# Moving the Silu blocks of a two-layer sequence kernel to the fifteenth slot of their units, with the products, softplus and tap sums around them

## The reference, cut to what matters

```
xn = layernorm(x) * (1 + scale) + shift          # scale, shift from silu(c) @ ada_w
x_in, z = split(xn @ in_proj_w.T)                # 1024 channels each
u  = silu(causal_conv4(x_in) + conv_b)           # 4 taps along the sequence
dt_r, B, C = split(u @ x_proj_w.T)               # 64, 16, 16 columns
dt = softplus(dt_r @ dt_proj_w.T + dt_proj_b)
for t:  h = h * exp(dt[t] * A) + dt[t] * u[t] * B[t];  y[t] = sum_n h[.., n] * C[t, n]
x1 = x + gate * ((y + u * D) * silu(z)) @ out_proj_w.T
```

## Time and profile before

| | |
|---|---|
| time, median of 3 runs | 2797.12 us (2796.01 to 2797.8) |
| the profiled execution's own time | 2798.95 us |
| its span, first to last instruction | 2797.2 us |
| before the first scan | 102.7 us |
| first layer's scans, 102.7 to 2198.3 | 2095.6 us |
| the rest: end of layer 1, layer 2 | 598.9 us |
| busy share of the span | PE 83%, DVE 83%, ACT 54%, POOL 65% |
| granted TensorE clock, mean | 0.923 of full speed |
| transfers | 178.2 MB, mean 64 GB/s |

### The profile page before, as it was taken

How to read it: one execution, slowest core, us unless ns; L and a number is a source line. 1 busy time by engine, 2 the same in 40 slices (tenths; PEclk the granted TensorE clock), 3 DMA queues, 4 the chain that set the end, 5 groups by cost and what they waited for, 6 DMA issues and landing times. The chain is left out here.

```text
span 2797.2 us, 23766 instructions
## 1 busy us (share of the span) xinstructions
PE 2332.3 (83%) x6868; PEld 1183.7 (42%) x6868; DVE 2309.3 (83%) x2514; ACT 1519.9 (54%) x3034; POOL 1818.4 (65%) x1119
## 2 busy tenths in 40 slices
PE   6788888888887888798889878887887699888988
PEld 2223333333333333233333333333332278767876
DVE  2698899889989988898899889988999566675667
ACT  4556656665666566556655665666555233332333
POOL 0377878887888788788878887888876412132203
PEclk9889899899989899999999999989988899999999
DMA  5410041013103100311041013002100121021103
GB/s 191 181 49 23 15 151 42 23 54 124 34 23 108 70 30 23 136 42 61 18 151 42 23 46 132 27 23 95 68 27 0 59 68 52 18 102 55 38 16 106
DMA packets 79040, 178.18 MB, mean 64 GB/s; under 512 B 7421, under 2 KB 10749, under 8 KB 78910
## 3 DMA queue, kind: packets, MB, share of 16 engines
q1 hardware_dynamic: 78910, 176.66, 18.6%
HBM read 159.33 MB, written 17.30 MB: 63 GB/s over the span
## 5 line engine op out<-in xcount | busy, mean ns | idle before, releaser
L1147 POOL TENSOR_TENSOR arena<-arena 128x1024 f32<-128x1024 f32 x512 | 1199.8, 2353 | 395.0 <-ACT arena L492 394.1
L803 DVE TENSOR_TENSOR_SCAN arena<-ps,arena 128x512 f32<-128x512 f32 x1024 | 1247.6, 1249 | 48.4 <-ACT ps L492 48.4
L259 PE MATMUL ps<-arena,keep 128*128 128x512 f32 x1760 | 932.4, 663 | 233.4 <-POOL arena L1147 191.0
L492 ACT ACTIVATE ps<-arena 128x512 f32<-128x512 f32 x1088 | 724.4, 680 | 456.8 <-DVE arena L803 421.2
L791 DVE TENSOR_TENSOR arena<-ps,arena 128x1024 f32<-128x1024 f32 x512 | 614.3, 1200 | 107.2 <-ACT ps L492 106.9
L259 PEld LDWEIGHTS ps<-arena,keep 128*128 128x128 f32 x1760 | 349.5, 207 | 756.5 <-issue 364.5
L218 PE MATMUL ps<-arena 128*128 128x512 f32 x1024 | 469.9, 607 | 14.8 <-issue 13.4
L492 ACT ACTIVATE arena<-arena 128x2 f32<-128x2 f32 (+2 forms) x697 | 234.9, 339 | 158.8 <-POOL arena L1099 86.8
L218 PEld LDWEIGHTS ps<-arena 128*128 128x128 f32 x1024 | 199.8, 197 | 284.9 <-issue 283.4
L246 PE MATMUL ps<-arena 128*128 128x512 f32 x512 | 233.8, 599 | 7.2 <-issue 6.4
L1121 POOL TENSOR_TENSOR arena<-arena 128x512 f32<-128x512 f32 x168 | 220.4, 1312 | 7.0
(11 more groups left out here) (110 smaller groups left out, 2496.4 us busy)
## 6 DMA issues: line engine op xcount, KB each, us to landing
arena<-scr_bc SPq DMA_DIRECT2D x128, 512.0 KB, 7.5
arena<-in_inT SPq DMA_DIRECT2D x128, 256.0 KB, 2.7
arena<-in_x SPq DMA_DIRECT2D x17, 512.0 KB, 3.7
scr_x<-arena SPq DMA_DIRECT2D x32, 256.0 KB, 2.0
arena_b<-scr_x SPq DMA_DIRECT2D x16, 512.0 KB, 3.6
arena_c<-scr_x SPq DMA_DIRECT2D x32, 256.0 KB, 2.7
out<-arena_c SPq DMA_DIRECT2D x32, 256.0 KB, 2.1
arena<-in_x SPq DMA_DIRECT2D x30, 256.0 KB, 3.3
```

The costliest lines, as they stand in the source:

```text
L259: last = e.matmul(YP, ident, hb[G % R][:, i, :], start=False, stop=(g == NG - 1 and i == n - 1))
L492: return e.activation(o_, i_, f, **kw)
L803: e.tensor_tensor_scan(H, DA[s % 4], H, h0, MUL, ADD).then_inc(v_sc)
L1147: m_ = e.tensor_tensor(H, H, BC[:, 16 + GN * g:16 + GN * g + GN, :], MUL)
```

## The change

The Silu blocks move from slot 11 to slot 14 of their units (in unit 6 from slot 10 to slot 12). Around them these move too:

- `z_mm`: slots 8 and 9 to slots 8 and 10;
- `dt_mm`: 4 to 5; `softplus`: 6 to 7; `add`: 8 to 9; `du`: 9 to 10 (each a slot later, in all units). `du_copy` stays in slot 13, but its code now stands ahead of the Silu blocks;
- `x_mm` of block 2: (4, 0) to (3, 15); block 3: (4, 5) to (4, 2); block 4: (4, 13) to (4, 10); block 6: (5, 14) to (5, 15). Evacuations and taps follow at their fixed distances: the evacuations are then at (3, 2), (3, 6), (4, 2), (4, 5), (4, 13), (5, 4), (6, 2), (6, 5), the taps of blocks 2, 3, 4 and 6 at (4, 3) to (4, 5), (4, 6) to (4, 8), (4, 14) to (5, 0) and (6, 3) to (6, 5);
- `proj`: (6, 12) to (6, 14); `proj_evac`: (7, 1) to (7, 3); `store_bc`: (7, 2) to (7, 4).

No instruction's shape and none's number changes.

```diff
@@ -143,10 +143,10 @@
-        XMM = {(2, 15): 0, (3, 3): 1, (4, 0): 2, (4, 5): 3, (4, 13): 4, (5, 1): 5, (5, 14): 6, (6, 2): 7}
+        XMM = {(2, 15): 0, (3, 3): 1, (3, 15): 2, (4, 2): 3, (4, 10): 4, (5, 1): 5, (5, 15): 6, (6, 2): 7}
         XEV = {after(k, 3): i for k, i in XMM.items()}
         TAP = {after(k, 4 + w): (i, 2 - w) for k, i in XMM.items() for w in range(3)}
-        SILU = {(3, 11): (0, 2), (5, 11): (2, 5), (6, 10): (5, 8)}
+        SILU = {(3, 14): (0, 2), (5, 14): (2, 5), (6, 12): (5, 8)}
@@ -160,8 +160,8 @@
-                if j % 2 == 1 and pr in (8, 9) and U + 1 < NU:
-                    V = U + 1 + pr - 8
+                if j % 2 == 1 and pr in (8, 10) and U + 1 < NU:
+                    V = U + 1 + (pr - 8) // 2
                     WSEQ.append((V // 8, 8 + V % 8))
@@ -286,13 +286,13 @@
-                    if U + 1 < NU and pr == 4:
+                    if U + 1 < NU and pr == 5:
                         dt_mm(U + 1)
-                    if U + 1 < NU and j % 2 == 1 and pr in (8, 9):
-                        z_mm(U + 1 + pr - 8)
+                    if U + 1 < NU and j % 2 == 1 and pr in (8, 10):
+                        z_mm(U + 1 + (pr - 8) // 2)
                     if more and (j, pr) in XMM:
                         x_mm(c + 1, XMM[j, pr])
-                    if more and (j, pr) == (6, 12):
+                    if more and (j, pr) == (6, 14):
                         proj(c + 1)
@@ -631,7 +631,7 @@
-                if U + 1 < NU and pr == 6:
+                if U + 1 < NU and pr == 7:
                     softplus(U + 1)
@@ -639,7 +639,7 @@
-                if more and j == 7 and pr == 1:
+                if more and j == 7 and pr == 3:
                     proj_evac(c + 1)
@@ -647,8 +647,10 @@
+                if U + 1 < NU and pr == 13:
+                    du_copy(U + 1)
                 silu = False
-                if U + 1 < NU and j % 2 == 1 and pr == 11:
+                if U + 1 < NU and j % 2 == 1 and pr == 14:
                     z_silu(U + 1)
                     z_silu(U + 2)
                     silu = True
@@ -657,8 +659,6 @@
                 if silu:
                     e.preload_act_table_set("natural_log_exp_and_others")
-                if U + 1 < NU and pr == 13:
-                    du_copy(U + 1)
@@ -850,7 +850,7 @@
-                if U + 1 < NU and pr == 8:
+                if U + 1 < NU and pr == 9:
                     add(U + 1)
@@ -1134,7 +1134,7 @@
-                if U + 1 < NU and pr == 9:
+                if U + 1 < NU and pr == 10:
                     du(U + 1)
@@ -1295,7 +1295,7 @@
-                if more and (j, pr) == (7, 2):
+                if more and (j, pr) == (7, 4):
                     store_bc(c + 1)
```

## The result

The changed kernel takes 2802.46 us (median of 20 runs, 2796.98 to 2805.89) beside 2795.93 us (20 runs, 2793.74 to 2797.99) before: a ratio of 1.0022, 95% interval 1.0016 to 1.0029. It is slower by a fifth of a per cent, where 2773 us and "faster" were forecast. One execution of experiment 10 took 2988.82 us at a mean granted clock of 0.737 and is left out of that experiment's median and ratio.

A forecast was written before the change was run, and what follows sets the result against it. VectorE's work sets the pace, with time lost at the Silu blocks. Five steady chunks (-3.9 each) -19.5, chunk 0 +0.7, chunk 4 +1.9, chunk 7 -6.9: -23.8 us, giving 2773 us beside the 2797.12 median; range 2746 to 2800.

The forecast's parts named there:

- Step 1: Unit 3: expand waits for du alone, 4.7 us left; the unit begins its successor at 34.8 instead of 35.97, -1.2 us.
- Step 3: Unit 5: GpSimd's taps done early, the whole expand wait goes by a 0.4 us margin; 29.1 instead of 37.96, -8.9 us.
- step 4: Unit 6: repeats unit 4's pattern, silu_u still ahead of du_copy; 35.7 instead of 35.79 us, -0.1 us.
- Step 2: Unit 4: late state copy and closer evacuations delay GpSimd, ScalarE and TensorE; 35.3 instead of 29.04 us, +6.3 us.
- Step 5: The rest: dt_mm costs nothing, softplus's new place mostly pays for later du; unit 1 0.4 more, unit 0 0.4 less.
- The sum: All chunks: five steady ones -19.5, chunk 0 +0.7, chunk 4 +1.9, chunk 7 -6.9, together -23.8 us.
- (b): Rival: waits only move, du is late wherever the block was, unit 5 wins no more than unit 4 loses; 2797, chance 0.10.
- (c): Rival, slower: GpSimd carries its lateness from unit 4 into unit 5, so du ends late there; 2810, chance 0.13.
- (a): Rival: unit 4 finds cover, about half of its 6.3 us loss goes, 3.2 in each of seven chunks; 2751, chance 0.20.
- (d): Rival: each of a Silu block's two table switches takes twice its row, 2.6 us more behind du_copy; 2835, chance 0.01.

The follow-up runs named there:

- experiment 10: Changed kernel with du in slot 9, keep_state before the Silu block, old x_mm slots, unit 6's block in slot 14, chunk 0's embedding columns in unit 4: 2735.04 us.
- Experiment 8: Kernel before the change with only the step-size chain one slot later (dt product 5, softplus 7, add 9, du 10): 2800.92 us, ratio 1.0017.
- experiment 7: Kernel before the change with only the Silu blocks in slot 14 (12 in unit 6) behind du_copy and the projection two slots later: 2764.65 us, ratio 0.9884.
- Experiments 2: Changed kernel with keep_state of slot 14 ahead of the Silu block instead of behind it: 2788.42 us, ratio 0.997.
- experiment 3: Changed kernel with the eight transposes of slot (1, 15) done over three times in slot (2, 0) on TensorE: 2787.68 us, ratio 0.9964.
- experiment 1: Changed kernel with du on GpSimd back in slot 9 instead of slot 10: 2761.68 us, ratio 0.9877.
- experiment 5: Changed kernel with chunk 0's second embedding column product and its use on VectorE moved from unit 3 to unit 4: 2795.45 us, ratio 0.9997.

## Why the prediction was wrong

**Step 1, unit 3,** was right to the row: 34.8 us worked out, 34.82 measured, the first expand waiting 4.66 us where 4.7 was worked out, behind a `du_copy` that waits for L1127. **Step 3** was right too (29.1 and 29.12 us), with block 4's evacuation out of the way, and **step 4** nearly (35.7 and 36.1).

**Step 2, unit 4,** named the right mechanism and sized it 0.7 to 1.5 us too low (35.3 against 36.0 to 36.8 in the steady chunks). In chunk 5 the term is block 4's evacuation, "over at 63.5, so it costs nothing": it is over at 66.4, counted from the same moment, while `du` ends at 65.2 where 65.1 was worked out. Its product comes late, since TensorE has waited 4.14 us for GpSimd before it and does the sums ahead of it at the lower clock (four records in 3.78 us again), so the evacuation and not `du` sets the copy.

**Step 5 failed, and with it the sign.** It set units 0, 1 and 2 at no change: the `mul` brought forward by softplus' new place was said to pay "for most of the `mul` that `du` now lets pass", and TensorE's work to keep its cost. Units 0 and 1 grow by 0.7 and 0.5 us: the first `mul` after softplus does come 1.8 us sooner (GpSimd's idle time before it in unit 0 falls from 4.8 to 2.95 us), but the next one then waits 0.76 us for its own state copy, and `du`, a whole `mul` of 2.3 us later in the order, ends after VectorE has arrived. Experiment 8, the chain alone, gives units 0 and 1 the same growth (0.7 and 0.5 us), and experiment 7, the blocks without the chain, none. Unit 2 grows by 1.6 us in chunks 2, 3 and 6, by 3.0 in chunk 5, and not at all in chunk 1. That was priced at nothing because each pace was taken from rows at the higher clock; the state copy behind the block of unit 1 opens a gap of 3 us on TensorE, and where the granted clock falls behind it, the sums that `y_fin` needs are slow. The gap by itself adds nothing there (chunk 1). Experiments 2 and 3 take the fall away in chunks 1 to 6, experiment 3 by nothing but work that fills the gap, and experiment 1 in all but chunks 2 and 6. Over the eight chunks units 0 to 2 lose 22.9 us where nothing was forecast; by these sums the scan phase would otherwise have come out some 19 us shorter than before.

**The sum** for chunk 0 failed by 4.7 us: +0.7 was forecast, +5.4 came. Units 0 to 2 are 5.2 of the miss. Unit 3 is 3.1: it grew by 1.9 us where -1.2 was forecast, since the product that only this chunk has between the two z products was not followed through the two banks, though a later Silu frees a bank later. Undoing that tie wins some 7 us (experiment 5), more than the 3.1; the kernel before had the same tie. Units 5 and 7 came out better than forecast. In all, the scan phase came out 27.4 us above the forecast: 19.1 from the five steady chunks (3.8 each, of which units 0 to 2 are 2.8 in chunk 3 and unit 4 0.8), 4.7 from chunk 0, 2.8 from chunk 4, 0.8 from chunk 7.

**The rivals.** The result lies nearest to (b), 2797 us, and by half of its mechanism: `du`, a `mul` later, is late wherever the block stands (experiment 1). But unit 5 won all of its wait, more than unit 4 lost, and what made up the difference, units 0 to 2, is not in (b). (c) was wrong, GpSimd starts unit 5 in time. (a) and (d) were wrong: unit 4 found no cover, and the block of unit 3 takes 4.6 us with two table loads of 1.28 and no gap behind either. The range ended 2.5 us below the median.

**What cost what.** The new place of the Silu blocks is a gain, 31 us by itself. With it, VectorE waits for `du` itself instead of for the block. In the new order `du` alone a slot later costs 41 us; in the old order the whole chain a slot later costs 5. In unit 3 the two can be compared: the old order loses nothing by it (34.97 us in experiment 8, 35.97 before), the new one 3.7 (34.82 us in the changed kernel, 31.09 in experiment 7), since there the block no longer hides the lateness. The totals don't compare so simply, since the 5 us are a difference of larger gains and losses.

## What to carry to other kernels

Where a wait is taken away, the one that ends second sets the new time, so a step that moves in the same change must be priced behind the new wait and not behind the old: here `du`, one multiplication later on GpSimd, gave back more than the Silu block's move had won (41 and 31 us). Whoever puts a long block on an engine should look at the small copies that come behind it, since a 0.2 us state copy held up GpSimd for 3 us, and TensorE with it. An idle stretch on TensorE may cost nothing as a wait and still cost 1.7 to 3 us by the lower clock behind it; what counts is whether the work behind it is waited for. And a chunk that differs from the others by one small product must be followed through the shared buffers on its own.

## What was not expected of the hardware

A wait of 3.03 us on TensorE, behind one of 1.61, was followed by a granted clock of 0.50 over the 3.9 us of the window shown, and doing 24 transposes for nothing in that gap made the program 16 us faster. Before the change the same place had a wait of 0.36 us and no fall, and the sums ahead of it had a wait of 1.94 us and one. The same two waits in chunk 1 of the changed kernel were followed by no fall, so the length of a wait alone doesn't tell. The Trainium skill, "Perfetto Trace Analysis", section "Matmul Optimizations", says that the matmul engine scales its power with its use and should get its matmuls back to back; the rows of chunk 5 agree, with 3.78 against 1.98 us for the same four records; those of chunk 1 show that one gap need not bring the lower clock about.
